# Row lists and sum matrices moved to ScalarE's queue, ten blocks joined into one, and one SyncE loop written out, in a two-network graph kernel

## The reference, cut to what matters

```python
# network 0: a graph ODE (RK4); every _gcn_conv is x @ W, a gather by src,
# a segment sum by dst with degree factors, and the node's own row
x = _l2norm(_gcn_conv(x, W1, b1, ...))
def f(z):
    z1 = _l2norm(_gcn_conv(z, Wf1, bf1, ...))
    return _gcn_conv(z1, Wf2, bf2, ...) + z
k1 = f(x); k2 = f(x + 0.5 * k1); k3 = f(x + 0.5 * k2); k4 = f(x + k3)
x = x + (k1 + 2.0 * k2 + 2.0 * k3 + k4) / 6.0
x = _gcn_conv(x, W2, b2, ...)
# network 1: attention over the same edges
kj = k[src] + e; vj = v[src] + e            # e = edge_attr @ We
alpha = einsum('ehc,ehc->eh', q[dst], kj) / sqrt(C)
alpha = segment_softmax(alpha, dst)
agg = segment_sum(vj * alpha, dst)
out = agg + x @ Wskip + bskip
x = layernorm(x + out + gelu(gelu(out @ W1 + b1) @ W2 + b2))
```

## Time and profile before

| | |
|---|---|
| median of 3 runs | 8550.52 us |
| profiled execution: time, span | 8565.12 us, 8563.4 us |
| scatter: first to last scatter issued | 261.1 to 806.3 us |
| coupled stages: first gather to the last stage's last inverse | 3059.1 to 7052.9 us |
| scores: first to last gather | 7061.8 to 7641.4 us |
| TensorE, VectorE, GpSimd, ScalarE busy | 74%, 72%, 64%, 45% of the span |

### The profile page before, as it was taken

The page is one execution under the profiler, slowest core; times in us unless marked ns, Lnnn a source line. Parts: engine busy times, 40 slices in busy tenths (PEclk is TensorE's granted clock), DMA queues, the critical chain, the costliest instruction groups (busy, mean ns, idle before and its releaser), DMA issues. The chain is left out here.

```text
span 8563.4 us, 164133 instructions
## 1 busy us (share of the span) xinstructions
PE 6367.4 (74%) x36634; PEld 5247.5 (61%) x36634; DVE 6158.6 (72%) x16609; ACT 3857.3 (45%) x10399; POOL 5467.9 (64%) x6135
## 2 busy tenths in 40 slices
PE   6000998889989965889898988989888665556666
PEld 2000888888888843667776666667655555554544
DVE  6420777778777888769777976887799883348976
ACT  9000675566666667653462156116522332233323
POOL 0566787777878766765575566557543656656667
PEclk7555999999999989999999999999999996778889
DMA  9453446765444456779778976987799663334444
GB/s 124 142 148 88 143 146 131 129 138 145 143 140 139 142 154 177 210 209 296 238 222 266 324 215 203 319 290 219 245 370 356 190 170 82 83 88 134 138 135 124
DMA packets 1714766, 1574.26 MB, mean 184 GB/s; under 512 B 172235, under 2 KB 1625659, under 8 KB 1714151
## 3 DMA queue, kind: packets, MB, share of 16 engines
q1 hardware_dynamic: 1287399, 986.98, 40.1%
q0 software_dynamic: 160192, 335.62, 14.8%
q10 hardware_dynamic: 266560, 244.12, 8.8%
HBM read 941.85 MB, written 624.58 MB: 183 GB/s over the span
## 5 line engine op out<-in xcount | busy, mean ns | idle before, releaser
L1251 PE MATMUL bank<-c_rows,sums_all 128*128 128x256 f32 (+1 forms) x3920 | 1301.3, 415 | 658.3 <-issue 335.4
L714 PE MATMUL bank<-wf_w,c_xt 128*128 128x256 f32 x6272 | 1564.7, 385 | 1.1 <-DVE y L1454 1.1
L1223 POOL DMA_INDIRECT c_rows<-t_tab,src_row x784 | 863.0, 1101 | 758.7 <-PE bank L1251 598.2
L1292 ACT ACTIVATE c_xt<-bank 128x512 f32<-128x512 f32 (+1 forms) x980 | 562.0, 573 | 1684.3 <-PE bank L1262 1160.4
L1389 DVE SCALAR_TENSOR_TENSOR c_rows<-bank,carry,c_rows 32x256 f32<-32x256 f32 (+1 forms) x1950 | 911.5, 467 | 529.4 <-PE bank L1251 261.6
L714 PEld LDWEIGHTS bank<-wf_w,c_xt 128*128 128x128 f32 x6272 | 1169.2, 190 | 188.0 <-ACT c_xt L1292 2.6
L1251 PEld LDWEIGHTS bank<-c_rows,sums_all 128*128 128x128 f32 x3920 | 655.7, 194 | 1024.1 <-issue 515.7
L1223 POOL DMA_INDIRECT c_rows<-z_tab,src_row x784 | 768.9, 981 | 299.4 <-issue 191.4
L1021 DVE TENSOR_TENSOR lx_lo<-bank,lx_hi 128x512 fp32r<-128x512 f32 (+1 forms) x1000 | 657.2, 657 | 342.7 <-ACT lx_hi L966 276.4
L966 ACT ACTIVATE lx_hi<-bank 128x512 fp32r<-128x512 f32 (+1 forms) x1000 | 561.4, 567 | 583.6 <-PE bank L935 456.7
L704 PE MATMUL bank<-wf_hi,lx_hi 128*128 128x256 f32 x3200 | 709.8, 303 | 94.9 <-issue 76.7
(11 more groups left out here) (327 smaller groups left out, 15875.8 us busy)
## 6 DMA issues: line engine op xcount, KB each, us to landing
c_z<-z_tab SPq DMA_DIRECT2D x882, 256.0 KB
z_tab<-lz SPq DMA_DIRECT2D x400, 256.0 KB
t_tab<-lt SPq DMA_DIRECT2D x400, 256.0 KB
z_tab<-y ACTq DMA_DIRECT2D x392, 256.0 KB
c_own<-z_tab SPq DMA_DIRECT2D x392, 256.0 KB
t_tab<-y ACTq DMA_DIRECT2D x392, 256.0 KB
c_own<-t_tab SPq DMA_DIRECT2D x392, 256.0 KB
xf_tab<-lxf SPq DMA_DIRECT2D x100, 256.0 KB
```

Source lines behind the costliest of these rows:

```text
L714: last = nc.tensor.matmul(out, x(k), w[:, k, :], start=(k == 0), stop=(k == ks - 1 and not bias))
L1223: pool.indirect_dma_start(out=rows[:, s, i, 0:XW] if first else rows[:, s, i, :], out_offset=None, in_=source, in_offset=bass.IndirectOffs ...
L1251: nc.tensor.matmul(psum[s % 2][:, i * win:(i + 1) * win], sums[:, j * 2 + i, :], rows[:, s, i, 0:win], start=True, stop=True).then_inc(S[" ...
L1292: nc.scalar.activation(xt[:, s % 2].rearrange("p k n -> p (k n)")[:, 0:n], psum[2 + s % 2][:, 0:n], ACT.Copy).then_inc(S["copied"], 1)
```

## The change

In the scatter, ScalarE's queue gets a program of its own with the row lists and the stores of sum matrices, in a loop; SyncE keeps only the 99 loads, written out. The ten coupled stages return their five engine programs instead of making a block each, and one block runs them in order; each engine's program of a stage but the first begins with waits (`settled`) until all stores of the stage before have landed. In the scores SyncE's program is written out, and within a turn the store of pair t - 2 comes ahead of the load of pair t + 3. The bodies of `coupled_stage` are otherwise the same and only lose a level of indentation; this is left out below.

```diff
@@ prepare: scatter @@
+                for j in range(turns):
+                    load(j, j % 4)
+
+            @block.scalar
+            def _(act):
                 def rows(j, s):
                     if isinstance(j, int) and j >= builds:
                         return
                     if not isinstance(j, int) or j >= 4:
-                        sp.wait_ge(S["row_floats"], pb.at("row_floats", j - 4))
-                    sp.dma_start(rows_i[:, s, :], a["dst_rows"][bass.ds(j * (4 * P), 4 * P)].partition_broadcast(P)
+                        act.wait_ge(S["row_floats"], pb.at("row_floats", j - 4))
+                    act.dma_start(rows_i[:, s, :], a["dst_rows"][bass.ds(j * (4 * P), 4 * P)].partition_broadcast(P)
                                  ).then_inc(S["sums_in%d" % s], 16)
 
                 def store(j, s):
-                    sp.wait_ge(S["sums_built"], pb.at("sums_built", j))
-                    sp.dma_start(m["sum_tab"][bass.ds(j * 4, 4), :, :].rearrange("t p f -> p t f"),
+                    act.wait_ge(S["sums_built"], pb.at("sums_built", j))
+                    act.dma_start(m["sum_tab"][bass.ds(j * 4, 4), :, :].rearrange("t p f -> p t f"),
                                  sums[:, s, :, :]).then_inc(S["stored%d" % s], 16)
-                skewed(sp, builds, [(0, load), (0, rows), (3, store)])
-                for j in range(builds, turns):
-                    load(j, j % 4)
+                skewed(act, builds, [(0, rows), (3, store)])
                 for s in range(4):
-                    sp.wait_ge(S["stored%d" % s], pb.ring_end("stored", s))
+                    act.wait_ge(S["stored%d" % s], pb.ring_end("stored", s))
@@ coupled_stages @@
-        coupled_stage(nc, S, counts, m, "first", 0, m["x_tab"], z[0], [])
+        stages = [coupled_stage(nc, S, counts, m, "first", 0, m["x_tab"], z[0], [])]
...
+        with nc.Block() as block:
+            @block.sync
+            def _(sp):
+                for sync_program, _, _, _, _ in stages:
+                    sync_program(sp)
...
@@ coupled_stage @@
-    with nc.Block() as block:
-        @block.sync
-        def _(sp):
+    stores = [] if first else [(f"stored{s}", ph.base[f"stored{s}"]) for s in range(4)]
+
+    def settled(eng):
+        for name, value in stores:
+            eng.wait_ge(S[name], value)
+
+    def sync_program(sp):
+        settled(sp)
...
+    return sync_program, gpsimd_program, tensor_program, scalar_program, vector_program
@@ scores @@
                     for part in range(3):
                         sp.dma_start(edge[part * ED:(part + 1) * ED, s, :],
-                                     a["edge_attr"][0:ED, bass.ds(j * (2 * P), 2 * P)]).then_inc(S[f"own_in{s}"], 16)
+                                     a["edge_attr"][0:ED, j * (2 * P):(j + 1) * (2 * P)]).then_inc(S[f"own_in{s}"], 16)
 
                 def store(j, s):
                     sp.wait_ge(S["values"], ph.at("values", j))
-                    sp.dma_start(m["v_tab"].rearrange("(t p) c -> p t c", p=P)[:, bass.ds(j * 2, 2), :],
+                    sp.dma_start(m["v_tab"].rearrange("(t p) c -> p t c", p=P)[:, j * 2:j * 2 + 2, :],
                                  values[:, s, :, :]).then_inc(S[f"stored{s}"], 16)
-                skewed(sp, pairs, [(0, load), (5, store)])
+
+                for j in range(pairs + 2):
+                    if j >= 2:
+                        store(j - 2, (j - 2) % 4)
+                    for n in ((0, 1, 2, 3) if j == 0 else (j + 3,)):
+                        if n < pairs:
+                            load(n, n % 4)
```

More of the change, by code:

```diff
@@ new lines, in gpsimd_program, with gather, invert @@
+    def gpsimd_program(pool):
+        settled(pool)
+        def gather(j, s):
+            if past(j, 4):
+                pool_wait(pool, S["summed"], ph.at("summed", j - 4), S["apart"])
+            which = m["src_row1"] if first else m["src_row"]
+            for i in range(2):
+                t = j * 2 + i
+                pool.indirect_dma_start(
+                    out=rows[:, s, i, 0:XW] if first else rows[:, s, i, :], out_offset=None, in_=source,
+                    in_offset=bass.IndirectOffsetOnAxis(ap=which[:, t:t + 1], axis=0)
+                ).then_inc(S[f"gathered{s}"], 16)
+        def invert(j, s):
+            pool_wait(pool, S["clamped"], ph.at("clamped", j), S["apart"])
+            nc.gpsimd.tensor_tensor(inv[:, s, :], ss[:, s, :], m["c_neg_half"][:], ALU.pow
+                                    ).then_inc(S["inverted"], 1)
+        if first:
+            nc.gpsimd.memset(m["c_neg_half"][:], -0.5).then_inc(S["c_constants"], 1)
+            pool.wait_ge(S["c_constants"], 1)
+        for j in range(pairs + (8 if rooted else 0)):
+            if j < pairs:
+                gather(j, j % 4)
+            if rooted and j >= 8:
+                invert(j - 8, j % 4)
@@ new lines, in tensor_program, with add_up, step, turn @@
+    def tensor_program(pe):
+        settled(pe)
+        def add_up(i):
+            def step(j, s):
+                pe.wait_ge(S["carried"], ph.at("carried", j, i + 1))
+                if i == 0:
+                    if first:
+                        pe.wait_ge(S[f"sums_in{s}"], ph.ring_at("sums_in", j, s))
+                    if past(j, 2):
+                        pe.wait_ge(S["u_set"], ph.at("u_set", j - 2))
+                nc.tensor.matmul(psum[s % 2][:, i * win:(i + 1) * win],
+                                 sums[:, j * 2 + i, :],
+                                 rows[:, s, i, 0:win], start=True, stop=True).then_inc(S["summed"], 1)
+            return step
+        def turn(j, s):
+            pe.wait_ge(S["u_set"], ph.at("u_set", j))
+            if past(j, 2):
+                pe.wait_ge(S["copied"], ph.at("copied", j - 2))
+            for k in range(ks):
+                for i in range(2):
+                    last = nc.tensor.transpose(psum[2 + s % 2][:, k * H2 + i * P:k * H2 + (i + 1) * P],
+                                               u[:, s % 2, i, k * P:(k + 1) * P], ident[:])
+            last.then_inc(S["turned"], 1)
+        def multiply(j, s):
+            pe.wait_ge(S["copied"], ph.at("copied", j))
+            if past(j, 2):
+                pe.wait_ge(S["taken"], ph.at("taken", j - 2))
+            if by_pe:
+                pe.wait_ge(S[f"degs_in{s}"], ph.ring_at("degs_in", j, s))
+            for i in range(2):
+                last = full_product(nc, psum[4 + s % 2][:, i * wout:(i + 1) * wout],
+                                    lambda k: xt[:, s % 2, k, i * P:(i + 1) * P], m[w + "_w"], ks,
+                                    (degs[:, s, i * P:(i + 1) * P], m["bf2_rows"][0:3, :]) if i in by_pe else None)
+            last.then_inc(S["product"], 1)
+        if turned_degs:
+            for k, tiles_ in enumerate((P, TE - P)):
+                last = nc.tensor.transpose(psum[6][0:tiles_, k * P:(k + 1) * P],
+                                           m["c_root_deg"][:, k * P:k * P + tiles_], ident[:])
+            last.then_inc(S["degs_turned"], 1)
+        skewed(pe, pairs, [(0, add_up(0)), (2, turn), (0, add_up(1)), (3, multiply)], unrolled=True)
```

550 lines of the change are left out of this document (251 added, 299 removed).

## The result

The changed kernel takes 8515.98 us (median of 9 runs, 8496.91 to 8538.22); the kernel before took 8550.47 us in the same comparison (9 runs, 8533.29 to 8561.55). The ratio is 0.9963, with a 95% interval of 0.9954 to 0.9972: 31.6 us less, with 24 to 39 us as its bounds. I had forecast 54 us less.

What follows compares the result with a forecast made beforehand. GpSimd's indirect DMAs were taken to set the pace in scatter, coupled stages and scores. Gains of 30 us (scatter), 24 (stage boundaries) and 0 (scores) make 54 off the 8550.5 us median: 8497 us, range 8440 to 8530.

Steps and rivals of the forecast that it cites:

- the case in which VectorE takes the load's place: Scatter rival: all 39 us come back as waits for VectorE's fill, only the boundaries count, 8526 us; chance 10%.
- the sign that I had set for being wrong: GpSimd waits in the scatter as often, but for VectorE's fill; or scores gathers come at 10.0 us per 8.
- Scatter, loads: SyncE, freed of row lists and stores, issues loads earlier; GpSimd's waits for them go, 30 us gained of at most 39.
- the 9 us taken off: Scatter: deduction from 39 us for turns in which VectorE, without GpSimd's pauses to catch up in, becomes late.
- Row lists and stores on ScalarE: Scatter: the same 98 DMAs issued by an engine idle there, each waiting only for VectorE; cost 0.
- the DMA share would do (0.68): Scatter: DMA engines, 0.61 busy before, still fit the same bytes in 30 us less, at 0.68.
- Coupled stages: Nine boundaries lose barrier, drain and branches; 4.0 to 4.8 us saved five times, 0.3 to 1.1 four times; 24 us taken.
- the whole 0.8 us that I had as its upper bound: Stage boundaries: first gather starts 0 to 0.8 us after the last store's semaphore.
- Scores: SyncE written out, store ahead of load: GpSimd waits for TensorE, not SyncE, so 0 gained, within -5 to +5 us.
- The written-out turns of before: Scores: SyncE's first 12 turns, already written out, gave 11.8 us per 8 gathers against 11.9 in its loop; 5 us at most.
- The loads did not starve: Scores rival: loads behind stores make edge rows late for ScalarE; at 1 us per pair 8595 us; chance 4%.
- The reference point: Whole kernel: sums made for the profiled execution of 8565.12 us, the same difference then taken off the median, 14.6 us lower.

Runs made afterwards that it cites:

- the second comparison: One-chip comparison of the kernel before with the scatter's, stages' or scores' part alone, and the changed kernel with VectorE's scatter program written out; kernel before 8538.28 us.
- the fourth: One-chip comparison of the kernel before again, the changed kernel with most list and store DMAs postponed or without comparisons, and one joining all helpful or harmless edits.
- no_cast_eight: Changed kernel with integer comparisons, eight slots instead of four, and VectorE's and GpSimd's scatter programs written out; 8492.51 us, ratio to before 0.9949.
- best: Changed kernel plus weights' split in the scatter's block, integer comparisons, eight slots, written-out scatter and scores programs; 8492.64 us, ratio to before 0.9927.

## Why the prediction was right, and where it was not

The predicted time was 8497 us; 8516 came, inside the range. The direction and the three places were right; one term of the sum was not. The range reached up to 8530 us, past the 8526 of the case in which VectorE takes the load's place, so the total within it says little for the scatter's term. There the sign that I had set for being wrong came out: GpSimd pauses about as often as before (9 times over 0.5 us, 10 before), mostly for the fill, and the last scatter is at 796 and not at 776.

*Scatter, loads: 30 us predicted, 13 us measured.* The removal itself was as computed: all ten waits went, 39 us. The step that failed is the 9 us taken off "for turns in which a VectorE without GpSimd's pauses to catch up in becomes late". That came to 32.4 - 13 x 0.30 = 28.5 us, so 10.5 us were left. First to last scatter shrank by 545.2 - 532.0 = 13.2 us; the rest is about what shorter scatters give (0.965 us in the mean instead of 0.973, 395 times). I had argued that at every wait of before the fill was earlier than the load. That was true and proves little. Pauses end VectorE's slow phases, as at 440.58, and without a wait for the load VectorE has not caught up when its next fill is due; that this is what made the fill early before fits the rows and was not tested by itself. The rival in which VectorE takes the load's place named what came; it set the return at 39 us and was nearer than my 9.

*Row lists and stores on ScalarE: 0 predicted, 2 us lost.* Four loads and four row lists now start together, and from the first load's issue to the first scatter it is 6.0 to 6.3 us in all ten kernels with this part, against 4.2 to 4.5 in the other four. (The first scatter is 2.9 us later, 264.05 against 261.13, of which 0.9 us is that its first load was issued later in that execution.) That the DMA share would do (0.68) was right. The net at the last scatter is 806.3 - 796.0 = 10.3 us.

*Coupled stages: 24 us predicted, about 24.* From store to gather 2.89 to 2.92 us everywhere, so 5 x 4.05 + 4 x 0.36 = 21.7 us, at the lower end of 21 to 28. The start behind the landing took nearly the whole 0.8 us that I had as its upper bound (4.8 - 4.05 = 0.75). The 2.5 us behind the last stage come on top; I had not seen them, so that 24 is met so closely is luck. The stretch shrank by 20.4 us (3993.8 to 3973.4); by the table it is 18 to 24 us in the second comparison and 13 to 17 us in the fourth.

*Scores: 0 predicted, 3 measured,* within -5 to +5. The written-out turns of before (11.8 us against 11.9) allowed for up to 5 us. The loads did not starve.

*The reference point.* I set the sum against one execution and carried it to the median. In that execution the local pass took 2252.8 us and the scores 579.7 us, the slowest of the table in both; the terms, which are differences within a stretch, did not suffer.

## What to carry to other kernels

When a wait is removed, ask what the pause did for the engine that is "early" at that wait: a producer that was ready in time only because its consumer had paused can be late once the pause is gone. Where several blocks follow one another, look at each block's end for drains and for blocks that need nothing of the one before; here they were worth some 24 and 17 us, more than the reordering of queues. And compare stretches over several executions before a difference in one of them is given a cause.

## What the runs showed of the hardware

- While GpSimd issues indirect DMAs back to back beside signals of other engines, these signals can come up to 9 us late, the one that an engine sends to itself included (443.78 to 452.62), and register instructions of VectorE take 0.70 us and not 0.06; in the rows shown the slow phase ends when GpSimd pauses. Beside the fills alone, from us 544 on, the longest of these pauses is 0.9 us. Written-out programs, fewer signals, more slots, less DMA traffic and less VectorE work each left 23 to 31 us of such waits in the scatter.
- In the scores the pause grows with the run of gathers: 2.0 us behind 8 (median), 2.4 to 2.7 us behind 12, in the changed kernel and with all programs written out.
- GpSimd's drain took 7.98 us at the end of the blocks of the first, mid and last stages before, 9.9 to 11.2 us behind the end stages, 2.1 us at the end of the joined block, and 12.4 us behind the scatter (9.1 and 8.6 us in the two kernels with GpSimd's scatter written out, no_cast_eight and best). What sets it is open.
